# Preparation of the first softmax attention on one Trainium2 core: one set of moments for two norms, normal rows and first parts on ScalarE

## What is computed

```python
def _L0_ffn_ref(x, ln1_g, ln1_b, ln2_g, ln2_b, wq, bq, wk, bk, wv, bv, wo, bo, gate_w, gate_b, w1, b1, w2, b2):
    ...
    hn = _layernorm(x, ln1_g, ln1_b)
    q = (hn @ wq + bq).reshape(b, s, NH, D).transpose(0, 2, 1, 3)
    k = (hn @ wk + bk).reshape(b, s, NH, D).transpose(0, 2, 1, 3)
    v = (hn @ wv + bv).reshape(b, s, NH, D).transpose(0, 2, 1, 3)
    scores = jnp.einsum('bhqd,bhkd->bhqk', q, k) / jnp.sqrt(jnp.float32(D))
    attn = jax.nn.softmax(scores, axis=-1)
    o = jnp.einsum('bhqk,bhkd->bhqd', attn, v)
    o = o.transpose(0, 2, 1, 3).reshape(b, s, h)
    x = x + (o @ wo + bo)
    ...
x = L0_attn_x
x = x + _L0_attn_ref(_layernorm(x, axis=-1), L0_attn_Wq, L0_attn_Wk, L0_attn_Wv, L0_attn_Wbeta, L0_attn_Wo, L0_attn_g_norm)
...
```

## Time and profile before

| | |
|---|---|
| runs | 2489.46, 2492.49, 2492.62 us (median 2492.49) |
| the profiled execution | 2492.9 us, its span 2491.1 us |
| instructions in the span | 55427 |
| busy: PE, DVE, ACT, POOL | 1942.5, 1705.4, 1193.1, 1125.1 us |
| granted PE clock, mean | 0.859 of 2.4 GHz |
| the stage of the change | from 455.7 us to 578.5 us of the span |

### The profile page before, as it was taken

One profiled execution on the slowest core, in us unless ns is written; L12 is line 12 of the kernel. 1 busy time (PEld: TensorE's weight loads), 2 busy tenths in 40 slices (PEclk: granted clock), 3 DMA queues, 4 the chain that ended last, 5 costly groups with the idle time before them and its releaser, 6 DMA issues. The chain is left out here.

```text
span 2491.1 us, 55427 instructions
## 1 busy us (share of the span) xinstructions
PE 1942.5 (78%) x18566; PEld 850.4 (34%) x18566; DVE 1705.4 (68%) x3077; ACT 1193.1 (48%) x2281; POOL 1125.1 (45%) x651
## 2 busy tenths in 40 slices
PE   4523554454999999658599779999999999999984
PEld 1212444320222222346344313333333333333333
DVE  5652311785777777364366468888888888888857
ACT  2320000012667777302166536666666666666654
POOL 3630001440000000263200148888888888888877
PEclk8757955565889999769799969999999999999995
DMA  1112000153111110411388732322222222223201
GB/s 37 16 20 36 4 4 4 42 156 86 35 36 38 38 38 25 126 50 48 93 277 285 247 81 76 80 70 69 68 68 77 76 69 68 68 69 80 73 6 43
DMA packets 239759, 179.76 MB, mean 72 GB/s; under 512 B 59636, under 2 KB 226676, under 8 KB 239236
## 3 DMA queue, kind: packets, MB, share of 16 engines
q1 hardware_dynamic: 228036, 172.31, 24.8%
q0 software_dynamic: 2304, 4.74, 0.6%
q10 hardware_dynamic: 9280, 0.79, 0.3%
HBM read 101.16 MB, written 75.26 MB: 71 GB/s over the span
## 5 line engine op out<-in xcount | busy, mean ns | idle before, releaser
L857 DVE TENSOR_REDUCE maxima_l<-max_l 128x1 f32<-128x512 f32 x1024 | 673.8, 685 | 119.4 <-PE max_l L933 108.8
L897 ACT ACTIVATE probs_l<-exp_l 128x512 f32<-128x512 f32 x1024 | 580.1, 599 | 320.7 <-PE exp_l L946 308.7
L830 POOL TENSOR_TENSOR part_sums_l<-probs_l 128x1024 f32<-128x1024 f32 x256 | 624.2, 2438 | 162.9 <-ACT probs_l L897 152.5
L933 PE MATMUL max_l<-k_stack_l,q_stack_l 96*128 96x512 f16 x1024 | 401.5, 392 | 42.5 <-DMA k_stack_l<-scratch_qk_l 25.5
L946 PE MATMUL exp_l<-q_stack_l,k_stack_l 100*128 100x512 f16 x1024 | 388.7, 382 | 0.0
L1140 DVE TENSOR_REDUCE maxima_l<-max_l 128x2 f32<-128x1024 f32 x256 | 305.8, 1222 | 93.0 <-PE max_l L1224 91.8
L1176 ACT ACTIVATE probs_l<-exp_l 128x512 f32<-128x512 f32 x512 | 282.8, 598 | 124.0 <-PE exp_l L1238 123.1
L981 PE MATMUL pv_bank_l<-probs_l,v_ring_l 128*32 128x512 f32 x2048 | 273.7, 606 | 0.3 <-issue 0.3
L933 PEld LDWEIGHTS max_l<-k_stack_l,q_stack_l 96*128 96x128 f16 x1024 | 99.0, 97 | 429.1 <-DVE maxima_l L857 382.9
L1578 POOL IOTA rows_e<- 128x32 int32 x1 | 0.2, 189 | 450.3 <-POOLq L26 450.3
L836 POOL TENSOR_TENSOR part_sums_l<-part_sums_l 128x512 f32<-128x512 f32 x128 | 183.2, 1431 | 10.0
(11 more groups left out here) (267 smaller groups left out, 2733.2 us busy)
## 6 DMA issues: line engine op xcount, KB each, us to landing
scratch_qk_l<-parts_g SPq DMA_DIRECT2D x128, 256.0 KB, 2.2
q_stack_l<-scratch_qk_l SPq DMA_DIRECT2D x192, 128.0 KB, 2.7
k_stack_l<-scratch_qk_l SPq DMA_DIRECT2D x192, 128.0 KB, 2.8
scratch_v_l<-v_g SPq DMA_DIRECT2D x32, 512.0 KB, 3.6
v_ring_l<-scratch_v_l SPq DMA_DIRECT2D x64, 256.0 KB, 3.0
scratch_stack_l<-parts_c SPq DMA_DIRECT2D x96, 128.0 KB, 2.3
q_stack_l<-scratch_stack_l SPq DMA_DIRECT2D x64, 96.0 KB, 2.1
k_stack_l<-scratch_stack_l SPq DMA_DIRECT2D x64, 96.0 KB, 2.1
```

The costliest lines, as they stand in the source:

```text
L830: pool.tensor_tensor(part_sums[:, i, h, :, :], probs[:, i, h, 0:2, :], probs[:, i, h, 2:4, :], ALU.add).then_inc(pair_sum.sem, 1)
L857: dve.reduce_max(maxima[:, s % 2, at % NT, at // NT:at // NT + 1], max_ps[at % 2][:, :], AX).then_inc(max_taken.sem, 1)
L897: act.activation(probs[:, i, at // NT, at % NT, :], exp_ps[exp_bank(s, at)][:, :], ACT.Exp, scale=a.scale).then_inc(prob_tile.sem, 1)
L933: pe.matmul(max_ps[at % 2][:, :], qs[0:SHIFT_ROW, s % RING, h, k * P:(k + 1) * P], ks[0:SHIFT_ROW, s % RING, h, :], start=True, stop=True) ...
```

## The change

The moments are taken once, of x. The variance of z follows from that of x and its rstd (var * rstd * rstd), and the mean of z is zero, so zn = x * scale + shift with scale = rstd_x * rstd_z. The moments of all batches are taken first, in three groups (`PREP_GROUPS`: batch 0, batches 1 to 3, batches 4 to 7). ACT makes the normal rows zn from x, hT from PSUM, and the first parts from PSUM with the bias; DVE makes the remainder from PSUM in one operation. All buffers are double, the eight PSUM banks are all used, the programs are written out without loops, SP stores the parts as they come, POOL stores v.

```diff
+PREP_GROUPS = ((0, 1), (1, 4), (4, B))
...
-            with sp.Fori(0, B // 2) as pair:
-                for i in range(2):
...
+            for b in range(B):
+                for part, (made_part, at) in enumerate(((part0, 1), (part1, 0), (part2, 0))):
+                    sp.wait_ge(made_part.sem, made_part.made(b, at))
                     for s in range(2):
                         for r, of in enumerate(a.pairs):
-                            sp.dma_start(scratch.stack[s].rearrange("(b g) h r d t -> b r (g h) d t", b=B)[b, r],
-                                         parts[:, i, s, of[s], :]).then_inc(parts_stored[i].sem, 16)
+                            if of[s] == part:
+                                sp.dma_start(stack[s, b, r], parts[:, b % 2, s, part, :]).then_inc(parts_stored[b % 2], 16)
...
+            def power(i, n):
+                pool.wait_ge(moments[i].sem, moments[i].made(n, 0))
+                size = tiles_of(n).stop - tiles_of(n).start
+                pool.tensor_tensor(rstd[:, i, tiles_of(n)], var[:, i, tiles_of(n)], g.minus_half[:, 0:size], ALU.pow).then_inc(rstd_ready[i].sem, 1)
+            power(0, 0)
+            power(1, 0)
+            power(0, 1)
+            power(1, 1)
+            pool.memset(v[:, :, :, :, :, a.width:L0_V], 1.0).then_inc(ones_built, 1)
+            power(0, 2)
+            power(1, 2)
+            pool.wait_ge(bo_loaded, 16)
+            for b in range(B):
+                tiles = slice(b * NT, (b + 1) * NT)
+                pool.wait_ge(z_ready.sem, z_ready.made(b, 0))
+                pool.tensor_tensor(g.z[:, tiles, :], g.z[:, tiles, :], bo[:, :].unsqueeze(1).broadcast_to([P, NT, D]),
+                                   ALU.add).then_inc(bo_added.sem, 1)
+                pool.wait_ge(v_ready.sem, v_ready.made(b, 0))
+                pool.dma_start(scratch.v.rearrange("(b g) p k h c -> b p g (k h c)", b=B)[b],
+                               v[:, b % 2, :, :, :, :].rearrange("p g k h c -> p g (k h c)")).then_inc(v_stored[b % 2], 16)
+            pool.wait_ge(bo_added.sem, bo_added.made(B - 1, 0))
+            for i in range(2):
+                pool.wait_ge(v_stored[i], 16 * (B // 2))
...
+            def moments_of_x(n):
+                tiles = tiles_of(n)
+                for k in range(tiles.start, tiles.stop):
+                    did(dve.bn_stats(stats[:, k, :], g.x[:, k, :]))
+                settle()
+                for k in range(tiles.start, tiles.stop):
+                    did(dve.bn_aggr(mv[:, k, :], stats[:, k, :]))
+                settle()
+                dve.tensor_scalar(var[:, 0, tiles], mv[:, tiles, 1], LN_EPS, None, ALU.add).then_inc(moments[0].sem, 1)
...
+            def moments_of_z(n):
+                tiles = tiles_of(n)
+                r = rstd[:, 0, tiles]
+                dve.wait_ge(rstd_ready[0].sem, rstd_ready[0].made(n, 0))
+                did(dve.tensor_tensor(var[:, 1, tiles], mv[:, tiles, 1], r, ALU.mult))
+                settle()
+                did(dve.tensor_tensor(var[:, 1, tiles], var[:, 1, tiles], r, ALU.mult))
+                settle()
+                dve.tensor_scalar(var[:, 1, tiles], var[:, 1, tiles], LN_EPS, None, ALU.add).then_inc(moments[1].sem, 1)
+                minus_mean_times(shift[:, 0, tiles], r, tiles).then_inc(z_scaled.sem, 1)
+            def scale_of_zn(n):
+                tiles = tiles_of(n)
+                dve.wait_ge(rstd_ready[1].sem, rstd_ready[1].made(n, 0))
+                did(dve.tensor_tensor(scale[:, tiles], rstd[:, 0, tiles], rstd[:, 1, tiles], ALU.mult))
+                settle()
+                minus_mean_times(shift[:, 1, tiles], scale[:, tiles], tiles).then_inc(zn_scaled.sem, 1)
+            def z(b):
+                for k in range(b * NT, (b + 1) * NT):
+                    last = dve.tensor_scalar(g.z[:, k, :], g.x[:, k, :], rstd[:, 0, k:k + 1], shift[:, 0, k:k + 1], ALU.mult, ALU.add)
+                last.then_inc(z_ready.sem, 1)
+            def remainder(b):
+                for s, bank in enumerate((q_bank, k_bank)):
+                    dve.wait_ge(part0.sem, part0.made(b, s))
+                    if b >= 1:
...
+                    dve.scalar_tensor_tensor(out=rest[:, s, :], in0=bank[b % 2][:, :], scalar=col[:, 2 + s:3 + s], in1=parts[:, b % 2, s, 0, :],
+                                             op0=ALU.add, op1=ALU.subtract).then_inc(rest_ready.sem, 1)
+            def values(b):
...
+                    last = dve.tensor_tensor(v[:, b % 2, :, k, :, 0:a.width], split(v_bank[b % 2][:, k * D:(k + 1) * D]), split(bv[:, :]), ALU.add)
+                last.then_inc(v_ready.sem, 1)
+            def last_part(b):
                 dve.wait_ge(part1.sem, part1.made(b, 0))
-                dve.tensor_tensor(parts[:, i, :, 2, :], qk[:, :, :], parts[:, i, :, 1, :], ALU.subtract).then_inc(part2.sem, 1)
+                dve.tensor_tensor(parts[:, b % 2, :, 2, :], rest[:, :, :], parts[:, b % 2, :, 1, :], ALU.subtract).then_inc(part2.sem, 1)
 
             moments_of_x(0)
-            normalise_x(0)
-            normalise_z(0, first=True)
+            moments_of_z(0)
             moments_of_x(1)
-            with dve.Fori(0, B // 2 - 1) as pair:
-                for i in range(2):
-                    step(pair * 2 + i, i, 2)
-            step(B - 2, 0, 1)
-            step(B - 1, 1, 0)
+            scale_of_zn(0)
+            moments_of_z(1)
+            moments_of_x(2)
+            scale_of_zn(1)
+            dve.wait_ge(qk_w_loaded, 16 * 6)
+            dve.wait_ge(v_w_loaded, 32)
+            dve.wait_ge(ones_built, 1)
+            for b in range(B):
+                if b == 0:
+                    moments_of_z(2)
+                z(b)
+                remainder(b)
+                if b == 0:
+                    scale_of_zn(2)
+                values(b)
+                last_part(b)
...
+            def normalised(b):
+                act.wait_ge(zn_scaled.sem, zn_scaled.made(group_of(b), 0))
+                if b >= 2:
+                    act.wait_ge(znT_ps.sem, znT_ps.made(b - 2, 0))
+                for k in range(NT):
+                    tile = b * NT + k
+                    act.activation(zn[:, b % 2, k, :], g.x[:, tile, :], ACT.Identity, bias=shift[:, 1, tile:tile + 1],
+                                   scale=scale[:, tile:tile + 1]).then_inc(zn_ready.sem, 1)
+            def affine(b):
+                act.wait_ge(znT_ps.sem, znT_ps.made(b, 0))
+                if b >= 2:
+                    act.wait_ge(v_ps.sem, v_ps.made(b - 2, 0))
+                act.activation(hT[:, b % 2, :], znT_bank[b % 2][:, :], ACT.Identity, bias=col[:, 1:2], scale=col[:, 0:1]).then_inc(hT_ready.sem, 1)
+            def first_part(b):
+                if b >= 2:
+                    act.wait_ge(parts_stored[b % 2], 16 * n_stores * (b // 2))
+                for s, bank in enumerate((q_bank, k_bank)):
+                    act.wait_ge(qk_ps.sem, qk_ps.made(b, s))
+                    act.activation(parts[:, b % 2, s, 0, :], bank[b % 2][:, :], ACT.Identity, bias=col[:, 2 + s:3 + s]).then_inc(part0.sem, 1)
+            def second_part(b):
+                act.wait_ge(rest_ready.sem, rest_ready.made(b, 1))
+                act.copy(parts[:, b % 2, :, 1, :], rest[:, :, :]).then_inc(part1.sem, 1)
+            normalised(0)
+            act.wait_ge(qk_w_loaded, 16 * 6)
+            affine(0)
+            for b in range(B):
+                if b + 1 < B:
+                    normalised(b + 1)
+                first_part(b)
+                if b + 1 < B:
+                    affine(b + 1)
+                second_part(b)
...
         @block.tensor
         def _(pe):
-            pe.wait_ge(w_loaded, 16 * 9)
             def transposes(b):
+                if b >= 2:
+                    pe.wait_ge(hT_ready.sem, hT_ready.made(b - 2, 0))
                 for k in range(NT):
                     pe.wait_ge(zn_ready.sem, zn_ready.made(b, k))
-                    ins = pe.transpose(znT_bank[:, k * P:(k + 1) * P], zn[:, k, :], g.ident[:, :])
-                ins.then_inc(znT_ps.sem, 1)
+                    last = pe.transpose(znT_bank[b % 2][:, k * P:(k + 1) * P], zn[:, b % 2, k, :], g.ident[:, :])
+                last.then_inc(znT_ps.sem, 1)
 
             def projections(b):
                 pe.wait_ge(hT_ready.sem, hT_ready.made(b, 0))
-                for s in range(2):
-                    pe.matmul(qk_bank[s][:, :], w[:, s, :], hT[:, :], start=True, stop=True).then_inc(qk_ps.sem, 1)
-                pe.wait_ge(v_ready.sem, v_ready.made_before(b, NT - 1))
+                if b >= 2:
+                    pe.wait_ge(rest_ready.sem, rest_ready.made(b - 2, 1))
+                for s, bank in enumerate((q_bank, k_bank)):
+                    pe.matmul(bank[b % 2][:, :], w[:, s, :], hT[:, b % 2, :], start=True, stop=True).then_inc(qk_ps.sem, 1)
+                if b >= 2:
+                    pe.wait_ge(v_ready.sem, v_ready.made(b - 2, 0))
                 for k in range(NT):
```

(38 more changed lines are left out.)

113 lines of the change are left out of this document (22 added, 91 removed).

## The result

The changed kernel was slower. Its executions had a median of 2511.5 us beside 2491.3 us of the kernel before; the ratio is 1.008, with a 95% interval of 1.0062 to 1.0098. I had forecast 2463 and a range that ended at 2474. The profiled execution took 2506.9 us with a span of 2505.2.

What follows compares the result with a forecast made beforehand. VectorE (DVE) was taken to set the stage's pace. First store at 478.4 plus 95 x 0.70 us put the last at 544.9 instead of 575.1, 30.2 us off 2492.9: 2462.7, forecast 2463, own range 2456 to 2470, whole range 2450 to 2474.

Steps and rivals of the forecast that it cites:

- All later stages run the same instructions: After the changed stage: nothing else changes, so the stage's 30.2 us come straight off the profiled 2492.9 us.
- my rivals: Five alternatives: faster store 0.14, longer ring of engine steps 0.11, POOL locked out 0.09, costly POOL store 0.04, no effect 0.02.
- the one that ended slower: POOL's v stores in the changed stage: at 12 us per store the kernel would take 2504 us; chance 0.04.
- DVE is no bound: VectorE in the changed stage: its work falls to 4.7 us per batch, so it no longer sets the pace.
- The start: Way to the stage's first store of 16-bit parts: at 478.4 us, 6.6 us earlier than before.
- SP sets the pace, 0.70 us a store: SyncE's store queue in the changed stage: 0.744 us a store becomes 0.70, so twelve take 8.4 us a batch.
- POOL's v store is hidden: POOL in the changed stage: additions and v store take 2.3 to 5.3 us per batch, below 8.4.
- It loses the eight v stores: SP's queue in the changed stage: v's stores move to POOL, part of SP's step to 0.70 us a store.
- Rival 3: POOL locked out while DVE works: POOL's period 10.0 us, stage gains only 19 us, kernel 2474 us; chance 0.09.
- The two halves of the buffer do not stop it: Buffer for parts: stores of batch b-2 land at most 3.3 us after last issue, while SP is busy with b-1.
- The sum for the stage: Last store of the changed stage starts at 544.9 instead of 575.1 us, 30.2 us less; the 3.34 us tail stays.

Runs made afterwards that it cites:

- e8: Changed kernel with 14 TensorE and 59 ACT semaphore increments ahead of the second attention, and v's store moved from POOL back to SP: 2459.0 us, ratio 0.9863.
- e3: Changed kernel with 14 semaphore increments on TensorE and 59 on ACT ahead of the second attention: 2458.3 us, ratio 0.9863.
- e6: Changed kernel with TensorE's and ACT's loops of the second attention written out turn by turn, no increments: 2455.9 us, ratio 0.9869.
- e4: Kernel before the change with 64 TensorE semaphore increments ahead of the second attention: 2492.3 us, ratio 0.9998.
- e5: Kernel before the change with 160 TensorE semaphore increments ahead of the second attention: 2523.0 us, ratio 1.0141.
- e9: Kernel before the change with 96 TensorE semaphore increments ahead of the second attention: 2488.3 us, one run.
- e10: Kernel before the change with 128 TensorE semaphore increments ahead of the second attention: 2500.9 us, one run.

## Why the prediction was wrong

**The step that failed** is one sentence of the sum: "All later stages run the same instructions." They do, and yet not from the same place. I took a stage's time as a property of its instructions and put what the change does to later stages at nothing; the second attention lost 52 us, one and two thirds of the gain of 31.1. None of my rivals held it: all five lay within the stage, and the one that ended slower put the loss on POOL's store. The sign would have been open to a reader of two things that I had: the page's instruction queues of the kernel before, which showed that a loop of 119 us a turn fetched nothing, and the order of the instructions, which showed PE's program growing by written-out batches ahead of it. The Trainium skill (Runtime: NRT & Kernel Launch, Instruction fetch mechanics) describes an instruction memory of 2048 instructions for TensorE, filled in blocks of 16 KB, or 256 instructions, and warns that a jump whose target is outside the current window of two pages stops the engine. The traces agree with the blocks of TensorE (16 KB in each packet of q8) and with the stop (2.94 and 3.74 us). They do not agree with the window of two pages, since TensorE's body of seven blocks ran six turns with no packet, nor with 16 KB for ACT, whose packets have 8. And they add what decided here: a body of 1634 instructions, under the size of the memory, is refetched or not according to where it begins.

**What held, in the prediction's own order:**
- *DVE is no bound.* It is busy 35.7 of 67 us; forecast was under 5 us a batch, and 35.7 / 8 = 4.5.
- *The start.* Forecast 478.4, measured 477.4, though this stage's first load came at 457.1, not at the 455.7 that the sum starts from, so that the start took 20.3 us, not 22.7; the power of twelve columns, taken as 2.3 us, took 2.27:

```profile
463.90 2.27 POOL L1353 TENSOR_TENSOR rstd_c<-var_c,minus_half 128x12 f32<-128x12 f32 x1 [2.53 <-DVE var_c L1394]
...
471.73 1.65 ACT L1472 ACTIVATE zn_c<-x_res,shift_c,scale_c 128x128 f32<-128x128 f32 x4 [4.50 <-DVE shift_c L1397]
```

- *SP sets the pace, 0.70 us a store.* The average was right and its parts were not. A written-out store starts 0.65 us after the last one, and in the changed kernel five of the 96 take 1.1 to 1.5 us. I had kept the 0.70 from the difference of two forms of a load; the two errors cancelled, which is luck.
- *POOL's v store is hidden.* It is so on POOL: 0.77 to 1.02 us, far under the 4.0 that I allowed for 512 rows. On SP it is not, as e8 shows. "It loses the eight v stores" is thus a term of SP's sum that was priced at a gain and was worth nothing. Rival 3, with its rule of the lock-out, did not come: v's stores keep their 0.77 us, and the additions take 1.25 us throughout.
- *The two halves of the buffer do not stop it.* ACT did wait, five times, for landings; SP had the other half's stores to issue meanwhile, so it cost nothing that the pace shows:

```profile
ACT parts_c L1486 <- DMA scratch_stack_l<-parts_c: 18.2, 5, 4.8
```

- *The sum for the stage*: 30.2 us less by forecast, 31.1 measured. With the loops in a good place or written out (e3: 2458.3; e6: 2455.9) the whole kernel comes to 5 to 7 us under the forecast of 2463, within its range.

Whether those 5 us are real, and where they come from, stays open. The forecast is 0.988 of the kernel before, and both intervals hold that ratio. From the first attention's first product to the second's, the changed kernel took 5.1 us less. The first attention's first and last product lie 407.5 us apart in the profiled execution of before and 401.4 in that after; e4, e5, e9 and e10, with before's preparation, have 402.9, 405.4, 404.1 and 402.2, and the runs with the new one 398.1 to 402.5. A part is thus what one execution differs from another, and the rest was not traced.

## What to carry to other kernels

When a change makes a program longer or shorter ahead of a large loop, the loop's place belongs to the change: compare the packets of the instruction queues per turn before and after, and look for waits on "issue" where the loop jumps back. If they appear, do not judge the change by the total: put the loop in a place where they are gone by increments of a semaphore, or write it out, and measure again. And take the number of instructions in a turn from the trace, not from a rule for how a product is compiled: mine was 9% too high and made a false exception of e4. A store that is moved to another queue, last, is not gone for the first: ask the first queue's own rows what the move saved.

## What I had not expected of the hardware

- TensorE fetches code in packets of 16 KB, and a loop of 1634 instructions runs with 0 or 9 packets a turn by where it begins: a body that ends 252 instructions into its seventh block is free, one that ends 28 into its eighth is refetched in two turns of six, and one that ends 60 into its eighth in every turn, at 28 us over six turns.
- A float32 transpose is one weight load and one matmul in the trace, a float32 product two of each.
- ACT's packets have 8 KB; its body of 305 instructions, five packets a turn, costs 30.5 us by itself.
- Straight code draws a packet every 21 us at no cost (e6: 943.3 us in the stage, as before with hardly any).
- After stops of 2.94 and 3.74 us TensorE's matmuls run at the 1.2 GHz pace (0.61 for 0.38 us), with a granted clock of 0.50 (0.87 over the stretch of 40 us); after the single stop of 2.80 us in e5 it is the same for 3.5 us.
- A plain store of 512 rows takes POOL 0.77 us, and of SP's issues the one that follows it by 1.3 to 1.9 us mostly takes 1.1 to 1.5 instead of 0.60 us.
